# Weight preparation in 128-row chunks, half of it and the block-level work moved into the feed-forward loop

## The chip, the cores and the metric

The kernel runs on all 8 cores of one Trainium2 chip, each core on its own two sequences of a batch of 16. The metric is the device time of the slowest core in microseconds (us). No core talks to another.

## What is computed

One layer: attention by blocks plus a feed-forward part, both on the layer-normed input. Per sequence: 2048 tokens (2 to a core, so 4096 rows on it), 1024 channels, 16 heads of 64. Blocks are 32 tokens, so 64 x 64 block pairs for each head, of which about 1024 are computed exactly and the rest by block means ("low").

```python
xn = layernorm(x)
Q, K, V = (heads(xn @ W.T + b) for W, b in ...)        # Wq, Wk, Wv
Qh, Kh, Vh = block means of Q, K, V over 32 tokens
low  = Qh Kh^T * scale;  row_max = low.max(-1)
norm = low - row_max + band * 5000
thresh = value of the 1024th largest of norm           # per head and sequence
hi_mask = norm >= thresh
hi  : softmax parts over the selected block pairs, exact
low : exp(low - row_max - 10000 * hi_mask) * 32, with Vh
attn = (hi_out * hi_corr + low_out * low_corr) / (norms + 1e-6)

xr, xk = mu * xn + (1 - mu) * shift(xn)                # mu_r, mu_k
ffn = sigmoid(xr @ Wr.T) * (square(relu(xk @ Wk2.T)) @ Wv2.T)
out = x + attn + ffn
```

## The kernel before

The program is one list of instructions in order of emission. `emit` puts an instruction on an engine's queue; for every engine but TensorE (PE) it first adds a wait for that engine's own last instruction. So VectorE (DVE) and ScalarE (ACT) run without overlap of their own, and the DMAs of one queue (SyncE's, SP, or GpSimd's, POOL) go one at a time: each waits until the one before it has landed. `wait` adds a wait for another engine's count. `barrier` makes every engine wait for all.

The stages, in the order of the trace:

1. **Layer norm** (L215 to L270): 32 tiles of 128 rows, transposed by PE into xnT, which holds all 4096 tokens of the core with channels on partitions.
2. **Weight preparation** (L274 to L331). DVE sums xnT over blocks (L275, eight reductions; L279 scales them into xnh). Then for each of the six weights: one POOL load of the whole matrix into wbuf (L286, f32 in DRAM, bf16 in SBUF), 64 PE transposes in groups of eight into two PSUM tiles (L295), a DVE copy after each group (L301), eight SP stores of 256 KB to the scratch wT_sc (L308). For q, k and v the block means are projected with the transposed weight while it is in SBUF: per d eight matmuls (L316) and a bias by DVE (L324), one group at a time. The next load waits for the last store.
3. **Block-level attention** (L345 to L401). For each of 32 heads and sequences: two small matmuls and five DVE instructions (low scores, L351 to L368), then a transpose, a copy and a memset (vhp, L379 to L384). Then 64 POOL transfers of 8 KB lay norm_all out over 128 partitions (nb128, L390 and L393), for which DVE waits.
4. **FFN with bisection** (loop `for Q in range(8)`, L537). One Q is 512 tokens. It has three passes, r, k2 and v2, of eight slices d; a slice is eight matmuls of 512 columns (L516) with a 256 KB weight slice that SP loads into a ring fW (`load_wslice`, L509). `wload(i)` waits until the slice that last used the buffer is through PE. Before the r and k2 passes DVE computes the mix (`mu_mix`, 12 us), after them ACT (sigmoid) or DVE (relu) takes the results; after the k2 pass ACT squares (L588); after the v2 pass PE transposes and POOL stores the result to part_sc (L614 to L626), and a barrier ends the Q. The threshold is found by 58 iterations of a bisection (`emit_bisect_iter`, L404 to L434: twelve DVE instructions with one PE sum in the middle), four after each mix, until they are used up in Q = 7.
5. **Selection masks** (`emit_sel_all`), and then the **attention** itself (from L640), 3.6 ms of it.

The lines that order a pass:

```python
                    r.wait("tensor", "sSY", wst["ld"][gi])
                    if d == 0:
                        r.wait("tensor", "sDV", ndv_mixr)
                    r.wait("tensor", "sAC", cons[par])
                    npe_q = mm_quarter("r", fA, d, fW[gi % 4], par)
                    wst["mm"][gi] = npe_q
                    wload(gi + 4)
```

Of the kernel before, what the change touches and what calls it, by code (L numbers as in the profile page):

```python
# [10 lines left out]
BF = mybir.dt.bfloat16  # L11
AF = mybir.ActivationFunctionType
ALU = mybir.AluOpType
# [82 lines left out]
def build_program(debug=False, trunc=None):  # L96
# [36 lines left out]
    with stack:  # L133
# [72 lines left out]
        with contextlib.ExitStack() as st_p0:  # L206
# [75 lines left out]
            st_w = contextlib.ExitStack()  # L282
            wbuf = st_w.enter_context(nc.sbuf_tensor("wbuf", [128, 8 * C], BF))
            wTsb = st_w.enter_context(nc.sbuf_tensor("wTsb", [128, 8 * C], BF))
            for tag in ("q", "k", "v", "r", "k2", "v2"):
                nld = r.emit("gpsimd", lambda e, s=w_in[tag]: e.dma_start(  # L286
                    wbuf.rearrange("p (a c) -> p a c", a=8),
                    s.rearrange("(a p) c -> p a c", p=128)))
                r.wait("tensor", "sGP", nld)
                wcons = [0, 0]  # L290
                for dc in range(8):
                    wpt = pT2[dc % 2]
                    r.wait("tensor", "sDV", wcons[dc % 2])
                    for cc in range(8):
                        r.emit("tensor", lambda e, dc=dc, cc=cc, wpt=wpt: e.transpose(  # L295
                            wpt[:, cc * 128:(cc + 1) * 128],
                            wbuf[:, dc * C + cc * 128:dc * C + (cc + 1) * 128],
                            id_bf[:, :]))
                    npe_w = r.cnt["sPE"]
                    r.wait("vector", "sPE", npe_w)  # L300
                    wcons[dc % 2] = r.emit("vector", lambda e, dc=dc, wpt=wpt: e.tensor_copy(  # L301
                        wTsb.rearrange("p (cc d) -> p cc d", cc=8)[:, :, dc * 128:(dc + 1) * 128],
                        wpt.ap().rearrange("p (cc x) -> p cc x", cc=8)))
                r.wait("tensor", "sDV", r.cnt["sDV"])
                ndv_wT = r.cnt["sDV"]
                r.wait("sync", "sDV", ndv_wT)
                for d in range(8):
                    nst = r.emit("sync", lambda e, tag=tag, d=d: e.dma_start(  # L308
                        wT_sc[tag][d].rearrange("(cc p) j -> p cc j", p=128),
                        wTsb.rearrange("p (cc x) -> p cc x", cc=8)[:, :, d * 128:(d + 1) * 128]))  # L310
# [929 lines left out]
```

How the kernel before makes its waits and increments, by code:

```python
    def emit(self, eng, fn):  # L57
        sname = ESEM[eng]
        n = 16 if eng in ("sync", "gpsimd") else 1
        if eng != "tensor" and self.cnt[sname]:
            self.wait(eng, sname, self.cnt[sname])
        self.cnt[sname] += n
        h = self.sem[sname]
        self._push(eng, lambda e, fn=fn, h=h, n=n: fn(e).then_inc(h, n))
        return self.cnt[sname]
# [1 line left out]
    def wait(self, eng, sname, val):  # L67
        if not val:
            return
        h = self.sem[sname]
        self._push(eng, lambda e, h=h, v=val: e.wait_ge(h, v))
```

## Time and profile before

| | us |
|---|---|
| median of the runs shown (5599.2 and 5612.5) | 5605.8 |
| the profiled execution | 5611.8 |
| its span, slowest core | 5610.2 |
| spans of the eight cores | 5577.4 to 5610.2 |
| busy in that span: PE, DVE, ACT, POOL | 3104.9, 2488.8, 1712.3, 286.4 |
| DMA moved | 181.7 MB, mean 32 GB/s |

The profiled execution is one execution; its span goes from the first to the last instruction of the slowest core. Each core's mean granted TensorE clock was 0.755 to 0.763 of full speed. In the rows below PE is TensorE's matmuls, PEld its weight loads, SPq the issues of SyncE's DMA queue, L and a number a line of the kernel. A row that groups several instructions of a queue gives the time from the first to the last of them.

### The profile page before, as it was taken

Reading aid. Unit: us, or ns where it says so; the run is one execution under the profiler, and the core shown is the slowest. Engines: PE = TensorE matmul, PEld = TensorE weight load, DVE = VectorE, ACT = ScalarE, POOL = GpSimd, SP = SyncE. Lnnn points to the kernel's source line nnn. Section 1 sums busy time; section 2 is a strip of 40 time slices with the busy share of each in tenths; the row PEclk is TensorE's granted clock in tenths of the full one; section 3 lists DMA queues with packets and bytes.
Section 4 is the critical chain, followed back from the end, with each engine's and each line's share of the span. In section 5 each row is a group of like instructions: output and inputs, shape, how many; then the busy total and the mean of one; then the engine's idle time right before and its main releaser. Section 6 shows DMA issues by size and latency. Waiting matters only on the chain.

```text
span 5610.2 us, 57324 instructions; the slowest of 8 cores (5577.4 to 5610.2 us)
## 1 busy us (share of the span) xinstructions
PE 3104.9 (55%) x11513; PEld 1106.3 (20%) x11513; DVE 2488.8 (44%) x5263; ACT 1712.3 (31%) x2627; POOL 286.4 (5%) x301
## 2 busy tenths in 40 slices
PE   1121203333333426776777776776776776777776
PEld 0011101111111111222222222222222122222122
DVE  3431304444444323653653653652752752743643
ACT  2300000000000002453453454354354355355245
POOL 0000020000000000000000000000000000000000
PEclk9965556666666766887787787788788788688678
DMA  1244001111222211100100100110110110110110
GB/s 59 64 75 89 24 4 38 45 47 47 49 53 53 57 42 27 29 18 19 31 18 12 35 18 16 28 24 16 23 29 15 25 29 13 26 29 4 29 21 16
DMA packets 516779, 181.70 MB, mean 32 GB/s; under 512 B 494282, under 2 KB 495474, under 8 KB 516274
## 3 DMA queue, kind: packets, MB, share of 16 engines
q1 hardware_dynamic: 482386, 130.46, 10.2%
q0 software_dynamic: 34080, 47.56, 4.7%
q8 instruction: 135, 2.21, 0.2%
q14 instruction: 178, 1.46, 0.1%
HBM read 142.23 MB, written 39.34 MB: 32 GB/s over the span
## 4 chain that ended last, share of the span: by engine, by line
PE 36%; DVE 22%; DMA 15%; ACT 13%; issue 10%; DVEq 1%; ACTq 1%; POOL 0%; POOLq 0%; SPq 0%
PE pS L850 9%; DVE bm L776 8%; ACT aT L865 7%; PE pO L818 7%; PE pA L765 7%; PE pA L1011 4%; PE pA L516 3%; PE pA L1072 2%; ACT stage L946 2%; DMA nb<-norm_all 2%; DMA fW<-wT_v 2%; DVE fA L501 2%; DMA fW<-wT_k 1%; DVE bis_ge L409 1%; DVE bis_cnt L413 1%
## 5 line engine op out<-in xcount | busy, mean ns | idle before, releaser
L776 DVE TENSOR_REDUCE bm<-pA 128x16 f32<-128x512 f32 x1664 | 1151.2, 692 | 608.4 <-PE pA L765 474.2
L865 ACT ACTIVATE aT<-pS 128x1024 bf16<-128x1024 f32 x1024 | 1049.7, 1025 | 775.5 <-PE pS L850 734.7
L818 PE MATMUL pO<-aT,vtm 128*65 128x512 bf16 x2048 | 702.6, 429 | 309.4 <-ACT aT L865 308.7
L765 PE MATMUL pA<-ktp,qtp 64*128 64x512 bf16 x1664 | 685.1, 423 | 311.1 <-ACT aT L865 110.1
L850 PE MATMUL pS<-rhsc,lhsc 128*128 128x512 bf16 x2048 | 718.0, 440 | 0.0
L516 PE MATMUL pA<-fA,fW 128*128 128x512 bf16 x1536 | 392.8, 419 | 147.0 <-DVE bis_hi L434 45.5
L417 PE MATMUL pB<-bis_cnt,ones 128*128 128x32 f32 x116 | 35.2, 397 | 688.3 <-DVE bis_cnt L413 688.3
L818 PEld LDWEIGHTS pO<-aT,vtm 128*65 128x65 bf16 x2048 | 234.8, 122 | 648.2 <-issue 500.0
L776 DVE TENSOR_REDUCE bm<-pO 128x16 f32<-128x512 f32 x384 | 265.6, 692 | 212.0 <-PE pO L765 177.2
L765 PEld LDWEIGHTS pA<-ktp,qtp 64*128 64x128 bf16 x1664 | 152.1, 95 | 880.7 <-issue 876.8
L1072 PE MATMUL pA<-xnT,wsl_v 128*128 128x512 bf16 x512 | 160.6, 470 | 136.5 <-DMA out<-stage 131.0
L765 PE MATMUL pO<-ktp,qtp 64*128 64x512 bf16 x384 | 188.4, 519 | 84.5 <-DMA bx<-bsm_dram 59.9
L516 PEld LDWEIGHTS pA<-fA,fW 128*128 128x128 bf16 x1536 | 157.8, 106 | 376.6 <-issue 241.4
L850 PEld LDWEIGHTS pS<-rhsc,lhsc 128*128 128x128 bf16 x2048 | 160.5, 107 | 316.0 <-issue 279.5
L558 ACT ACTIVATE fR<-pA 128x512 bf16<-128x512 f32 x64 | 38.3, 598 | 588.0 <-PE pA L516 588.0
L558 ACT ACT_TABLE_LOAD x1 | 1.3, 1283 | 605.4 <-PE pA L516 605.4
L588 ACT ACTIVATE fA<-fB 128x512 bf16<-128x512 bf16 x64 | 40.4, 631 | 422.8 <-DVE fB L581 417.7
L417 PEld LDWEIGHTS pB<-bis_cnt,ones 128*128 128x128 f32 x116 | 29.1, 311 | 697.3 <-issue 697.3
L888 DVE TENSOR_TENSOR rdenw<-pS,eps_all 128x8 f32<-128x8 f32 x16 | 2.7, 167 | 366.4 <-PE pS L881 365.5
L1011 PE MATMUL pA<-xnT,wsl_q 128*128 128x512 bf16 x512 | 123.0, 386 | 67.2 <-DMA wsl_v<-wT_v 65.7
L946 ACT ACTIVATE stage<-pA,rdenw 128x64 f32<-128x64 f32 x384 | 121.5, 316 | 67.7 <-DVE rdenw L936 34.2
L785 DVE TENSOR_TENSOR bmm<-bm,bx 128x64 f32<-128x64 f32 x512 | 115.6, 226 | 54.2 <-DVE bm L776 1.4
(150 smaller groups left out, 2536.3 us busy)
## 6 DMA issues: line engine op xcount, KB each, us to landing
xtile<-x SPq DMA_DIRECT2D x64, 512.0 KB
fW<-wT_r SPq DMA_DIRECT2D x64, 256.0 KB
fW<-wT_k SPq DMA_DIRECT2D x64, 256.0 KB
fW<-wT_v SPq DMA_DIRECT2D x64, 256.0 KB
out<-stage SPq DMA_DIRECT2D x32, 512.0 KB
rhsc<-qtp POOLq DMA_DIRECT2D x32, 256.0 KB, 3.5
lhsc<-ktp POOLq DMA_DIRECT2D x32, 256.0 KB, 2.9
bx<-bsm_dram POOLq DMA_DIRECT2D x32, 256.0 KB, 7.8
```

The lines of the kernel that those rows point to most:

```text
L417: npe_c = r.emit("tensor", lambda e: e.matmul(pB1[:, :], ones128[:, :], bis_cnt[:, :], start=True, stop=True))
L501: e.scalar_tensor_tensor(d[:, c * QT:(c + 1) * QT], xnT[:, base:base + QT], mucol[m][:, c:c + 1], d[:, c * QT:(c + 1) * QT], ALU.mult, ALU ...
L516: e.matmul(pA[:, sl * 512:sl * 512 + QT], w[:, cc * 128:(cc + 1) * 128], rb[:, cc * QT:(cc + 1) * QT], start=(cc == 0), stop=(cc == 7)))
L765: e.matmul(pap, qtp[p0:p0 + 64, ts0 + t * 128:ts0 + (t + 1) * 128], ktp[p0:p0 + 64, ts0 + kq * 512:ts0 + (kq + 1) * 512], start=True, stop ...
L776: e.tensor_reduce(bmp[:, kq * 16:(kq + 1) * 16], pap.rearrange("p (k e) -> p k e", e=32), axis=AX.X, op=ALU.max))
L785: e.tensor_tensor(bmm[:, :], bmp[:, :], bx2[bpar][:, t * 64:(t + 1) * 64], ALU.add))
L818: e.matmul(pO[0:65, sl * 512:(sl + 1) * 512], vtm[:, (sq * 16 + k) * 130 + hip * 65: (sq * 16 + k) * 130 + hip * 65 + 65], aT[bpar][:, sl ...
L850: e.matmul(pS[bpar][:, sl * 512:(sl + 1) * 512], lhs2[par][:, k * 128:(k + 1) * 128], rhs2[par][:, qh * 1024 + sl * 512: qh * 1024 + (sl + ...
L865: e.activation(aT[bpar][:, :], pS[bpar][:, :], AF.Exp, scale=0.125))
L946: e.activation(stg[:, i * 64:(i + 1) * 64], pA[:, sl8 * 128:sl8 * 128 + 64], AF.Identity, scale=rdenw16[:, i:i + 1])))
L1011: e.matmul(pA[:, slot * 512:(slot + 1) * 512], wsl[tag][:, cc * 128:(cc + 1) * 128], xnT[:, cc * T + n * 512:cc * T + (n + 1) * 512], star ...
L1072: e.matmul(pA[:, slot * 512:(slot + 1) * 512], wsl["v"][:, cc * 128:(cc + 1) * 128], xnT[:, cc * T + n * 512: cc * T + (n + 1) * 512], sta ...
```

## The change

Three things are edited, all in stages 2 to 4.

- The whole-matrix buffers wbuf and wTsb give way to two chunk buffers wbuf2 and one wTsb2, each 128 x 1024. `wpd_load` loads 128 rows of a weight on POOL; `wpd_proc` transposes them, copies, stores the slice to wT_sc and, for q, k and v, projects the block means with it. Only r, k2 and v2 are now prepared ahead of the FFN, and the barrier behind the preparation is gone.
- q, k, v, the low blocks, the vhp blocks, nb128 and the bisection are put in a list of 24 sites, three in each Q: `do_site(Q * 3)` behind the r pass, `+ 1` behind the k2 pass, `+ 2` behind the v2 pass and its stores, ahead of the barrier. Sites 2 to 13 prepare two chunks each, 11 to 14 compute eight low blocks each, 15 all vhp blocks and nb128, 16 to 23 eight iterations of the bisection each (23: the last two).
- The ring fW has three buffers instead of four, and prefetches run three slices ahead.

```diff
+            def wpd_load(tag, d):
+                g = wp["g"]
+                wp["g"] = g + 1
+                r.wait("gpsimd", "sPE", wp["npe"].get(g - 2, 0))
+                wp["nld"][(tag, d)] = r.emit(
+                    "gpsimd", lambda e, tag=tag, d=d, g=g: e.dma_start(
+                        wbuf2[g % 2][:, :], w_in[tag][d * 128:(d + 1) * 128, :]))
...
+            def wpd_proc(tag, d):
+                nld, g = wp["nld"][(tag, d)]
                 r.wait("tensor", "sGP", nld)
...
+                r.wait("tensor", "sAC", r.cnt["sAC"])
                 r.wait("tensor", "sDV", r.cnt["sDV"])
+                wpt = pT2[g % 2]
...
+                npe_w = r.cnt["sPE"]
+                wp["npe"][g] = npe_w
+                r.wait("vector", "sPE", npe_w)
+                r.wait("vector", "sSY", wp["nst"])
+                nwc = r.emit("vector", lambda e, wpt=wpt: e.tensor_copy(
+                    wTsb2[:, :], wpt[:, :]))
+                r.wait("sync", "sDV", nwc)
+                wp["nst"] = r.emit("sync", lambda e, tag=tag, d=d: e.dma_start(
+                    wT_sc[tag][d].rearrange("(cc p) j -> p cc j", p=128),
+                    wTsb2.rearrange("p (cc x) -> p cc x", cc=8)))
                 if tag in ("q", "k", "v"):
...
+                r.wait("tensor", "sDV", r.cnt["sDV"])
+
+            for tag in ("r", "k2", "v2"):
+                wpd_load(tag, 0)
+                wpd_load(tag, 1)
+                for d in range(8):
+                    wpd_proc(tag, d)
+                    if d + 2 < 8:
+                        wpd_load(tag, d + 2)
...
             fW = [st_p0.enter_context(nc.sbuf_tensor(f"fW{j}", [128, 8 * 128], BF))
-                  for j in range(4)]
+                  for j in range(3)]
...
-                if i - 4 >= 0:
-                    r.wait("sync", "sPE", wst["mm"][i - 4])
+                if i - 3 >= 0:
+                    r.wait("sync", "sPE", wst["mm"][i - 3])
                 tag, d = wsched[i]
-                wst["ld"][i] = load_wslice(fW[i % 4], tag, d)
+                wst["ld"][i] = load_wslice(fW[i % 3], tag, d)
...
+            for j, tag in enumerate(("q", "k", "v")):
+                base = 2 + j * 4
+                for ch in range(4):
+                    for d2 in (0, 1):
+                        d = ch * 2 + d2
+                        addw(base + ch,
+                             lambda tag=tag, d=d: wpd_proc(tag, d))
+                        if d + 2 < 8:
+                            addw(base + ch,
+                                 lambda tag=tag, d=d: wpd_load(tag, d + 2))
+                nxt = {"q": "k", "k": "v", "v": None}[tag]
+                if nxt is not None:
+                    addw(base + 3, lambda nxt=nxt: wpd_load(nxt, 0))
+                    addw(base + 3, lambda nxt=nxt: wpd_load(nxt, 1))
+            for j, si in enumerate((11, 12, 13, 14)):
+                for bb in bh_list[j * 8:(j + 1) * 8]:
+                    addw(si, lambda bb=bb: emit_low_bh(*bb))
+            for bb in bh_list:
+                addw(15, lambda bb=bb: emit_vhp_bh(*bb))
+            addw(15, emit_nb128)
+            for si in range(16, 24):
+                for it in range((si - 16) * 8, (si - 16) * 8 + 8):
+                    if it < N_BISECT:
+                        addw(si, lambda it=it: emit_bisect_iter(it))
...
+            wpd_load("q", 0)
+            wpd_load("q", 1)
+            r.wait("vector", "sPE", r.cnt["sPE"])
             for Q in range(8):
                 t0 = Q * QT
                 mu_mix(fA, "r", t0)
                 ndv_mixr = r.cnt["sDV"]
-                for itq in range(4):
-                    it = Q * 8 + itq
-                    if it < N_BISECT:
-                        emit_bisect_iter(it)
...
-                    npe_q = mm_quarter("r", fA, d, fW[gi % 4], par)
+                    npe_q = mm_quarter("r", fA, d, fW[gi % 3], par)
                     wst["mm"][gi] = npe_q
-                    wload(gi + 4)
+                    wload(gi + 3)
...
+                do_site(Q * 3 + 0)
                 r.wait("vector", "sPE", r.cnt["sPE"])
                 mu_mix(fA, "k", t0)
```

`emit_low_bh`, `emit_vhp_bh` and `emit_nb128` hold the instructions of L345 to L401 as they were; the first two begin with PE waits for everything that ACT and DVE have been given so far.

## Rows read from the trace of the kernel before

**Rows 1.** The page: its span line, and the chain that ended last, by engine.

```profile
span 5610.2 us, 57324 instructions; the slowest of 8 cores (5577.4 to 5610.2 us)
...
PE 36%; DVE 22%; DMA 15%; ACT 13%; issue 10%; DVEq 1%; ACTq 1%; POOL 0%; POOLq 0%; SPq 0%
```

**Rows 2.** Windows by stage: stretch, then busy us per engine, clock, DMA share, GB/s.

```profile
284.70:594.10 309.40, 59.81 (x576) 47.96 (x576) 77.72 (x82) 0.00 (x0) 5.32 (x6) 0.62 0.44 82
594.10:845.40 251.30, 30.02 (x160) 19.89 (x160) 43.34 (x226) 0.00 (x0) 33.49 (x64) 0.50 0.03 7
845.40:2001.40 1156.00, 446.15 (x1908) 201.53 (x1908) 505.46 (x1142) 79.95 (x129) 15.73 (x29) 0.69 0.21 49
2001.40:5610.20 3608.80, 2535.86 (x8608) 811.49 (x8608) 1759.37 (x3484) 1547.92 (x2369) 231.03 (x197) 0.79 0.11 22
```

**Rows 3.** Timeline of w_k's preparation: start us, us, engine, line, instruction, [idle before].

```profile
370.53 1.01 PE L295 MATMUL pT<-id_bf,wbuf 128*128 128x128 bf16 x8 [28.33 <-DMA wbuf<-w_k]
...
378.60 19.58 SPq L308 DMA_DIRECT2D wT_k<-wTsb  x8
...
401.08 0.87 POOL L286 DMA_DIRECT2D wbuf<-w_v  x1 [47.73 <-DMA wT_k<-wTsb]
```

**Rows 4.** Timeline of TensorE and ScalarE in the first r and k2 passes.

```profile
884.26 14.61 PE L516 MATMUL pA<-fA,fW 128*128 128x512 bf16 x56 [3.17 <-DVE bis_hi L434]
...
956.33 1.89 PE L516 MATMUL pA<-fA,fW 128*128 128x512 bf16 x8 [1.22 <-DMA fW<-wT_k]
...
959.29 5.69 ACT L588 ACTIVATE fA<-fB 128x512 bf16<-128x512 bf16 x8 [57.02 <-DVE fB L581]
```

**Rows 5.** Timeline of SyncE's queue, same r pass: first and last of five issues.

```profile
887.97 0.36 SPq L509 DMA_DIRECT2D fW<-wT_r  x1
...
899.46 0.36 SPq L509 DMA_DIRECT2D fW<-wT_k  x1
```

**Rows 6.** Timeline at the borders: block means done, low blocks, vhp blocks, first mix.

```profile
321.02 0.69 DVE L279 TENSOR_SCALAR xnh<-sq_dump 128x1024 bf16<-128x1024 f32 x1
...
594.17 0.44 PE L351 MATMUL pA<-khT,qhT 64*64 64x64 f32 x2 [23.10 <-DMA wT_v<-wTsb]
...
673.73 0.28 PE L379 MATMUL pA<-id_f,vhT 64*64 64x64 f32 x1 [1.81 <-DVE rm_all L368]
...
845.45 0.06 DVE L487 MEMSET fA<- 128x1 bf16 x1 [138.73 <-DMA nb<-norm_all]
```

**Rows 7.** DMA issues: destination<-source, queue, count, KB each, us to landing.

```profile
wbuf<-w_k POOLq DMA_DIRECT2D x2, 2048.0 KB, 17.5
...
wbuf<-w_q POOLq DMA_DIRECT2D x1, 2048.0 KB, 17.4
...
nb<-norm_all POOLq DMA_DIRECT2D x64, 8.0 KB, 1.6
```

**Rows 8.** Timeline after the first v2 pass, and the landing of ptile's stores.

```profile
994.13 0.69 DVE L622 COPY ptileb<-pTb 128x1024 bf16<-128x1024 bf16 x1 [2.60 <-DMA part_sc<-ptileb]
...
1000.47 0.35 DVE L496 TENSOR_SCALAR fA<-xnT,mucol1m_r 128x512 bf16<-128x512 bf16 x1 [5.64 <-DMA part_sc<-ptileb]
...
DMA to landing us min/median/max: 2.3/2.5/4.2
```

**Rows 9.** Timeline of one group of head matmuls and its bias.

```profile
341.19 1.01 PE L316 MATMUL pA<-xnh,wTsb 128*128 128x128 bf16 x8 [0.68 <-DVE qhT L324]
342.38 0.35 DVE L324 TENSOR_SCALAR qhT<-pA,bcol_q 128x128 f32<-128x128 f32 x1 [1.33 <-PE pA L316]
```

**Rows 10.** Timeline: first instruction of two bisection iterations that follow each other.

```profile
870.77 0.19 DVE L405 TENSOR_TENSOR bis_mid<-bis_lo,bis_hi 128x32 f32<-128x32 f32 x1
...
877.21 0.19 DVE L405 TENSOR_TENSOR bis_mid<-bis_lo,bis_hi 128x32 f32<-128x32 f32 x1
```

**Rows 11.** Windows: the end of a k2 pass, and the head matmuls of w_k.

```profile
953.00:958.30 5.30, 3.77 (x16) 1.42 (x16) 1.08 (x2) 0.00 (x0) 0.00 (x0) 1.00 0.41 95
382.00:391.00 9.00, 5.35 (x43) 3.89 (x41) 1.85 (x6) 0.00 (x0) 0.00 (x0) 0.50 0.39 101
```

More of the change, by code:

```diff
@@ L280, in build_program @@
                 xnh[:, :], sq_dump[:, :], 1.0 / BLK, None, ALU.mult))
[L282 to L288, printed above, removed]
-                r.wait("tensor", "sGP", nld)
[L290 to L303, printed above, removed]
-                r.wait("tensor", "sDV", r.cnt["sDV"])
[L305 to L310, printed above, removed]
@@ new lines, in build_program @@
+            wbuf2 = [st_p0.enter_context(nc.sbuf_tensor(f"wbuf{j}", [128, C], BF))
+                     for j in range(2)]
+            wTsb2 = st_p0.enter_context(nc.sbuf_tensor("wTsb2", [128, C], BF))
+            wp = {"nld": {}, "npe": {}, "nst": 0, "wc": [0, 0], "g": 0}
+            def wpd_load(tag, d):
[5 more added lines that the diff above has]
+                        wbuf2[g % 2][:, :], w_in[tag][d * 128:(d + 1) * 128, :]))
+                wp["nld"][(tag, d)] = (wp["nld"][(tag, d)], g)
@@ L328, in build_program @@
-                r.wait("gpsimd", "sSY", nst)
-                r.wait("gpsimd", "sDV", r.cnt["sDV"])
-            r.barrier()
-            st_w.close()
+                    r.wait("tensor", "sDV", max(ndvh, nwc))
+                    for cc in range(8):
+                        r.emit("tensor", lambda e, cc=cc: e.matmul(
+                            pA[:, 0:128],
+                            wTsb2[:, cc * 128:(cc + 1) * 128],
+                            xnh[:, cc * 128:(cc + 1) * 128],
+                            start=(cc == 0), stop=(cc == 7)))
@@ new lines, in emit_nb128 @@
+            def emit_nb128():
+                ndv_n = r.cnt["sDV"]
+                r.wait("gpsimd", "sDV", ndv_n)
+                for b in range(NBH):
+                    r.emit("gpsimd", lambda e, b=b: e.dma_start(
+                        nb128[0:64, b * 32:(b + 1) * 32],
+                        norm_all[0:64, b * 64:b * 64 + 32]))
+                    r.emit("gpsimd", lambda e, b=b: e.dma_start(
+                        nb128[64:128, b * 32:(b + 1) * 32],
+                        norm_all[0:64, b * 64 + 32:b * 64 + 64]))
+                ngp_n = r.cnt["sGP"]
+                r.emit("vector", lambda e: e.memset(bis_lo[:, :], -100000.0))
+                r.emit("vector", lambda e: e.memset(bis_hi[:, :], 100000.0))
+                r.wait("vector", "sGP", ngp_n)
@@ L563, in build_program @@
                 ndv_mixk = r.cnt["sDV"]
-                for itq in range(4, 8):
-                    it = Q * 8 + itq
-                    if it < N_BISECT:
-                        emit_bisect_iter(it)
                 consd = [r.cnt["sDV"], r.cnt["sDV"]]
```

143 lines of the change are left out of this document (68 added, 75 removed).

## The prediction

> **What bounds the kernel now.** I read the spans and clocks of all cores first (5577 to 5610 us, one clock, so nothing is disturbed), then the busy times by stage, then the timeline of the first 2000 us, and the issues of SyncE's DMA queue last. The span is 5610.2 us, and no engine fills it: the chain that ended last is PE 36%, DVE 22%, DMA 15%, ACT 13% [rows 1]. By stage [rows 2]: from 284.7 to 594.1 the weights are prepared, to 845.4 stands the block-level attention, to 2001.4 the feed-forward part (FFN) with the bisection, and the last 3609 us are the attention, which the change does not touch. So at most about 1.7 ms is in play. Up to 2001 us this is a serial chain: every engine waits for its own last instruction, and at most steps for another engine. A piece of work that is moved costs as much in the new place, unless it finds there something to lie beside.
>
> The preparation is a case of waiting on transfers: of the 48.6 us from one load to the next (the idle 47.7 and the issue 0.9) some 18 are the load, 8 transposes and copies, 20 the eight stores [rows 3]. In the FFN, by contrast, a pass of 64 matmuls is already close to its weight loads. In the pass at 884.26 the first slice (8 matmuls) takes 3.7 us at half clock, and only then is its buffer free and the fifth slice's load issued; the following five issues (first and last shown) stand 2.87 us apart, in the next pass 3.0; the last slice starts after a DMA wait of 1.2 us [rows 4, 5]. With P = 2.95 us a load, the model 3.7 + 4 x 2.95 + 0.1 + 1.9 = 17.5 us gives the pass; 884.26 to 901.5 is 17.3, 940.4 to 958.2 is 17.8. All 24 passes end in this way.
>
> **The change, part by part.**
>
> (a) r, k2 and v2 are prepared by 128-row chunks. It still begins when DVE has the block means, at 321.7, and before the change the whole preparation ends at 594.2: 272.5 us [rows 6]. Afterwards 24 chunks run as a pipeline. Two limits: the store loop (one wTsb2: the copy, 0.7, waits for the previous store to land; 19.6 us for eight stores are 2.74 each [rows 3]) gives 3.6 us a chunk. The load loop (POOL, one at a time): the full load lands in 17.5 us and an 8 KB one in 1.6 [rows 7], so an eighth is 1.6 + 15.9/8 = 3.6, plus 0.5 issue, 4.15. POOL's stores beside other traffic took up to 4.2 us to landing where 2.5 is the median [rows 8]; the chunks run beside the stores, so up to 1.5 more. I take 4.5, between 3.6 and 5.65. 1.3 + 22 x 4.5 + 1.9 = 102 us, so the FFN begins at about 424. The term is -170 (-191 to -145).
>
> (b) q, k and v go to 12 sites in the FFN, two chunks each. One chunk on the chain: transposes 1.2 until the copy, copy 0.7, 0.25 to the head matmuls, 1.2 to the bias, 0.35, and 0.15 back: 3.8 us [rows 3, 9]. But the second copy waits for the first chunk's store, and this is queued on SyncE behind the last three weight prefetches. When a pass ends, the first of these has been in flight for 2 us; the store is issued at +6.9 and lands at +9.7; copy, matmuls and bias bring the site's end to +12.3. After the r pass DVE began the next mix at +0.2, so each of those four sites costs 12.1. After the k2 pass the squares began 1.1 us after its end [rows 4]; ACT now waits for the site: 11.3, four times. After the v2 pass PE's wait for DVE lets the site begin only after the last copy at 994.8; the prefetches are through by then, and the two chunks end at 1002.6 instead of the mix at 1000.5 [rows 8]. Behind them on POOL are the last store and two chunk loads of 4.15 each, for which the end-of-Q barrier waits: 1008.6, so 8.1, three times; at the fourth the low blocks cover the loads: 2.1. Sum: 48.4 + 45.2 + 24.3 + 2.1 = +120.
>
> (c) The 32 low blocks (2.49 us each, 594.17 to 673.73), the vhp blocks and the 64 nb128 transfers (138.7 us of DVE waiting [rows 6]) are moved, at nothing gained: PE waits for everything before them, and DVE stands before the k mix of Q = 5 just as it stood before Q = 0. What would cover nb128 is other DVE work, and there is none behind it in the queue. Only at the one v2 site that holds low blocks alone do they lie beside the last store, which took 5.6 us [rows 8]: -5. One second wait, for the last sigmoid: +1. Term -4.
>
> (d) The 58 iterations stay, 6.43 us each [rows 10]. They move from "behind the mix" to "behind the pass". After an r pass DVE's first four instructions (3.2 us) run during the pass (two sites); after a v2 pass 5.6 us of store lie under them (three sites); eight groups for fifteen save some hand-overs. -27.
>
> (e) The ring of fW goes from four buffers to three. By the model above slice 3 is now the first to wait for the end of slice 0: five loads instead of four stand between the first slice and the last. Each pass is P = 2.95 longer, and what follows each pass waits for its end: 24 x 2.95 = +71. Lower bound 0, if loads became quicker; upper in the rivals.
>
> The removed barrier is worth nothing. Sum: -170 + 120 - 4 - 27 + 71 = -10. Against the profiled execution's own time (5611.8 us, 1.6 us outside its span) that is 5602; it stood 6 us above the median of the runs shown, 5605.8, so I say 5596.
>
> The trace also bears on what a chunk load costs by rule: an 8 KB transfer on POOL took 1.6 us and the full load 17.5 [rows 7]. The Trainium skill, "DMA: Bandwidth & Descriptors" (Anatomy of one DMA), gives such a DMA about 2.0 us fixed and the bytes at 436 GB/s; for 512 KB that would be an estimated 3.2 us, the store loop would be the limit, and the sum -30 instead of -10. The full load by the same rule would be 11.6 us and took 17.5, so the rows decide.
>
> **Rivals.**
>
> *The clock falls in the thinned passes.* With three buffers PE works 1.75 us of each 2.95 us at the end of a pass, for four slices in a row instead of two. For: the head matmuls, 5.4 us busy in 9.0, ran at 0.50 of the clock throughout [rows 11]. Against: from 953.0 to 958.3, with two such gaps, it stayed at 1.00 [rows 11], and at the low clock a slice of 8 takes 3.41 us, which fills the interval, so it would rise again. If it falls once a pass: the last slice ends 1.9 later, 24 x 1.9 = +46, 5642. If from the fourth slice on all run at half clock, a pass takes 8 x 3.41 = 27.3 instead of 20.5: 24 x 6.8 = +163, 5759, slower by more than 2%. This is the case on the other side; it decides from +122, about 5 us a pass. The Trainium skill, "TensorE: Matmul & The Clock Gate" (HAM oscillation), describes just such a kernel, whose clock fell at every weight tile because PE waited for the next tile's transfer; the waits there were longer than the 1.2 us of these rows, and the trace does not agree so far.
>
> *The prefetch is not the limit.* If the loads ran closer together once there is one less in flight, (e) is worth 0: 5525. Against: they are already one at a time, each waiting for the one before. If besides the store of a site were not held up behind the prefetches (8 sites x 4.7 = 38), 5487, faster by over 2%.
>
> *The chunk loads are slow.* 6 us a load would put 33 us on the preparation and 3 x 3.7 on the barriers: 5640. Against: the two loads shown took 17.4 and 17.5, and the first of them (w_q) ran under DVE's block sums [rows 7]. The Trainium skill, "SBUF — State Buffer" (the "DVE blocks DMA" trap), says a DMA issued from GpSimd can be held up by some DVE instructions; no row here shows it.
>
> **How the numbers follow.** Forecast 0.60 (its own range 5565 to 5625: the bounds of (a)); clock once a pass 0.11; clock through the pass 0.06; ring free 0.08; ring and store free 0.08; slow chunk loads 0.07. A measurement of this kernel can tell about 2% (112 us) from no change. Faster by over 2%: 0.08. Slower: 0.06. Within: 0.86. The range leaves out the two outer cases: 5525 to 5650.
>
> **What would show it.** The timeline: the first r mix at 415 to 435, where it stood at 845.4. In each pass five prefetches about 2.95 apart before the last slice starts 18.6 us after the first; a pass takes 20.5. Granted clock 1.00 in the second half of passes. Weight sites of 12 us after r and k2 passes, with DVE's copy waiting for a wT store; at the end of Q 0 to 3 a barrier that waits for wbuf loads. DVE still idle 138.7 us for nb, now in Q = 5. The attention stage unchanged at 3609. I am wrong if passes stay at 17.6, if the clock is 0.5 late in passes, or if nb128 lies beside other work.

## The result, and the profile after

The changed kernel takes 5665.8 us (median; 5656.9 to 5670.2), the kernel before, run beside it, 5600.65. The ratio is 1.0112, 95% interval 1.0099 to 1.0124: slower by 1.1%. I had forecast a gain of 10 us (5596, range 5525 to 5650): the class "within 2%" holds, the sign and the range don't.

The profiled execution took 5657.2 us. First the page's span and chain, then the windows by stage (columns as in [rows 2]; the preparation, everything up to the masks, and the attention):

```profile
span 5655.6 us, 57782 instructions; the slowest of 8 cores (5626.3 to 5655.6 us)
...
PE 35%; DVE 22%; DMA 17%; ACT 14%; issue 11%; DVEq 1%; ACTq 1%; POOL 0%; SPq 0%; POOLq 0%
```

```profile
284.70:440.70 156.00, 24.27 (x192) 18.57 (x192) 52.14 (x33) 0.00 (x0) 13.77 (x26) 1.00 0.46 81
440.70:2080.80 1640.10, 528.15 (x2452) 248.44 (x2452) 575.38 (x1419) 79.76 (x129) 62.14 (x118) 0.66 0.19 44
2080.80:5655.60 3574.80, 2520.67 (x8608) 808.20 (x8608) 1757.84 (x3482) 1543.43 (x2369) 230.55 (x194) 0.79 0.11 22
```

The chain has more DMA than before (17% for 15%, [rows 1]) and less PE. All the difference is made by the moment at which DVE begins stage 5, "masks begin" from here on. Its row in the changed kernel's timeline:

```profile
2080.77 0.18 DVE L451 COPY thr<-bis_lo 128x32 f32<-128x32 f32 x1 [0.19 <-DVE bis_hi L446]
```

As the mean over the eight cores of each profile, masks begin at 2002.0 before and 2065.6 after: +64, as the times have it (+65). What is behind it lasts 3587 us before and 3576 after; over all the kernels below that figure lies between 3576 and 3593 in no order, so I take it for scatter. On core 5, which both profiles show, masks begin at 2011.9 and at 2080.8: +69, where my sum had -10. Its row in the kernel before:

```profile
2011.88 0.18 DVE L439 COPY thr<-bis_lo 128x32 f32<-128x32 f32 x1 [5.00 <-DMA part_sc<-ptileb]
```

[rows 2] puts the border at 2001.4, while the last copies and stores of the loop still run; the 3609 us that the prediction gives the attention hold 10.5 us of them. From masks to the end core 5 takes 3598 us before and 3575 after. Against the forecast 79 us have to be found, all of them in stages 2 to 4.

**The preparation** (answers to [rows 3, 6, 7]). Timeline of the changed kernel: start, us, engine, line, instruction, [idle before].

```profile
284.86 0.57 POOL L292 DMA_DIRECT2D wbuf<-w_r  x1 [282.61 <-DVE xnT L267]
289.56 0.54 POOL L292 DMA_DIRECT2D wbuf<-w_r  x1 [4.13 <-DMA wbuf<-w_r]
...
333.22 0.53 POOL L292 DMA_DIRECT2D wbuf<-w_r  x1 [4.62 <-DMA wbuf<-w_r]
333.75 0.69 DVE L311 COPY wTsb<-pT 128x1024 bf16<-128x1024 bf16 x1 [4.41 <-DMA wT_r<-wTsb]
...
440.72 0.06 DVE L499 MEMSET fA<- 128x1 bf16 x1
```

The first r mix is at 440.7, where I said 415 to 435. A chunk load alone leaves its queue idle for 4.13 us behind the issue (4.2 from the start of the issue to the landing), beside the stores for 4.6 to 4.8 (4.5 to 4.6 to the landing); that is a cycle of 5.1, not 4.5. DVE, too, waits 4.4 us for a store whose whole cycle was 2.7 when nothing ran beside it [rows 3]: the two loops slow each other and end up at the same pace.

**A pass** (answers to [rows 4, 5]). TensorE in the first k2 pass, then two windows of it, the pass at 485.86 and the tail of one at 1970 (columns as in [rows 2]):

```profile
485.86 9.45 PE L528 MATMUL pA<-fA,fW 128*128 128x512 bf16 x32 [12.46 <-DVE fA L513]
495.71 1.89 PE L528 MATMUL pA<-fA,fW 128*128 128x512 bf16 x8 [0.41 <-DMA fW<-wT_k]
498.73 1.89 PE L528 MATMUL pA<-fA,fW 128*128 128x512 bf16 x8 [1.12 <-DMA fW<-wT_k]
501.76 1.89 PE L528 MATMUL pA<-fA,fW 128*128 128x512 bf16 x8 [1.15 <-DMA fW<-wT_k]
504.88 1.89 PE L528 MATMUL pA<-fA,fW 128*128 128x512 bf16 x8 [1.23 <-DMA fW<-wT_k]
...
1975.25 3.36 PE L528 MATMUL pA<-fA,fW 128*128 128x512 bf16 x8 [2.43 <-DMA fW<-wT_k]
```

```profile
500.00:507.50 7.50, 4.39 (x19) 1.52 (x17) 1.94 (x3) 0.00 (x0) 0.00 (x0) 1.00 0.43 98
...
1975.25:1979.00 3.75, 3.36 (x8) 0.96 (x8) 0.21 (x1) 0.00 (x0) 0.00 (x0) 0.54 0.31 72
```

Four slices of this pass wait for their weights, spaced 3.0, and the clock stays at 1.00 (2.4 GHz) in these gaps: the tail of a pass is as drawn. The 24 passes last 508.6 us together, before 425.2: +83 where I had +71. Core 5 is the worst of the eight here; as the mean over the cores it is 500.7 for 425.0, +76. The slice at 1975.25 ran at a clock of 0.54 (the lower level), after a wait of 2.43 us, twice the usual. On this core one more late slice did, and one behind a wait as long did not:

```profile
1797.93 3.53 PE L528 MATMUL pA<-fA,fW 128*128 128x512 bf16 x8 [2.35 <-DMA fW<-wT_v]
...
1120.11 1.89 PE L528 MATMUL pA<-fA,fW 128*128 128x512 bf16 x8 [2.33 <-DMA fW<-wT_k]
```

**A weight site** (to be set against [rows 8, 9]). Between the r and the k2 pass of Q = 1; the pass ends at 590.87. The row with x3 holds the three prefetches.

```profile
588.81 9.63 SPq L521 DMA_DIRECT2D fW<-wT_k  x3
...
592.72 0.69 DVE L311 COPY wTsb<-pT 128x1024 bf16<-128x1024 bf16 x1 [22.72 <-PE pT L303]
593.08 0.53 POOL L292 DMA_DIRECT2D wbuf<-w_q  x1 [37.35 <-PE pT L303]
...
598.14 0.53 POOL L292 DMA_DIRECT2D wbuf<-w_q  x1 [4.53 <-DMA wbuf<-w_q]
602.98 3.90 SPq L314 DMA_DIRECT2D wT_q<-wTsb  x2
605.70 0.69 DVE L311 COPY wTsb<-pTb 128x1024 bf16<-128x1024 bf16 x1 [11.01 <-DMA wT_q<-wTsb]
```

The mechanism is the predicted one: DVE's second copy waits for the first chunk's store, and that stands behind three prefetches. But from the first prefetch (588.81) to the store (602.98) are 14.2 us, 4.7 each, where I had 2.95. The store is issued 12.1 after the pass, not 6.9. While a prefetch and a chunk load both move bytes, the DMA engines are nearly full. The DMA view from 593.2 to 598.1: 40 slices of 0.12 us, the busy share of the 16 engines in tenths (9 is 90% or more), and the share of GpSimd's queue over the whole window:

```profile
DMA  0000000026641034497897998999997899520000
...
q0 software_dynamic: 144, 0.26, 29.5%
```

**The moved block work** (answers to [rows 6]). A vhp block, and the first instruction of the k mix behind nb128:

```profile
1290.79 0.28 PE L389 MATMUL pA<-id_f,vhT 64*64 64x64 f32 x1 [0.94 <-DVE vhp_all L394]
...
1434.68 0.35 DVE L508 TENSOR_SCALAR fA<-xnT,mucol1m_k 128x512 bf16<-128x512 bf16 x1 [142.57 <-DMA nb<-norm_all]
```

DVE still stands idle for nb128, 142.6 us against 138.7, as said, in Q = 5. A vhp block takes 1.22 us instead of 1.01.

### The profile page after: what moved, and what is told of

Its sections match the earlier page's. It is cut to its first block, busy times and chain, and to the rows that moved or that the text cites. A ratio compares the mean times of both kernels' runs of the same rounds, so it can differ in the third digit from the quotient of the medians.

```text
span 5655.6 us, 57782 instructions; the slowest of 8 cores (5626.3 to 5655.6 us)
## 1 busy us (share of the span) xinstructions
PE 3106.1 (55%) x11513; PEld 1100.6 (19%) x11513; DVE 2488.9 (44%) x5263; ACT 1707.4 (30%) x2627; POOL 307.3 (5%) x343
## 4 chain that ended last, share of the span: by engine, by line
PE 35%; DVE 22%; DMA 17%; ACT 14%; issue 11%; DVEq 1%; ACTq 1%; POOL 0%; SPq 0%; POOLq 0%
PE pS L896 9%; DVE bm L822 8%; ACT aT L911 7%; PE pO L864 7%; PE pA L811 7%; PE pA L1057 4%; DMA fW<-wT_k 3%; DMA fW<-wT_v 3%; PE pA L1118 2%; ACT stage L992 2%; PE pA L528 2%; DMA fW<-wT_r 2%; DMA nb<-norm_all 2%; DVE fA L513 2%; DVE bis_ge L421 1%
## 5 line engine op out<-in xcount | busy, mean ns | idle before, releaser
L528 PE MATMUL pA<-fA,fW 128*128 128x512 bf16 x1536 | 405.1, 421 | 536.2 <-DVE fA L513 343.1
L1035 POOL TENSOR_TENSOR stage<-stage,xtile 128x1024 f32<-128x1024 f32 x32 | 74.9, 2340 | 1237.3 <-ACT stage L992 659.0
L836 DVE TENSOR_REDUCE mv_all<-bmm 128x1 f32<-128x64 f32 x512 | 112.7, 220 | 55.1 <-DVE bmm L831 3.0
```

Source lines behind the costliest of these rows:

```text
L528: e.matmul(pA[:, sl * 512:sl * 512 + QT], w[:, cc * 128:(cc + 1) * 128], rb[:, cc * QT:(cc + 1) * QT], start=(cc == 0), stop=(cc == 7)))
L836: e.tensor_reduce(mv_all[:, b * 16 + t:b * 16 + t + 1], bmm[:, :], axis=AX.X, op=ALU.max))
```

## The experiments

All compare with the kernel before run on the same chip. "Gap" is the time from the end of one pass to the start of the next. Passes and gaps are those of the core with the longest span in each profile; where the mean over the eight cores tells something else, it is given.

| | median us | ratio, 95% interval | masks begin, mean of cores | 24 passes, us |
|---|---|---|---|---|
| before | 5600.65 | 1 | 2002.0 | 425.2 |
| changed | 5665.8 | 1.0112 (1.0099 to 1.0124) | 2065.6 | 508.6 |
| e1 changed, ring of 4 | 5618.6 | 1.0006 (0.9981 to 1.0031) | 2019.0 | 428.7 |
| e2 before, ring of 3 | 5682.5 | 1.0125 (1.0089 to 1.016) | 2072.7 | 504.2 |
| e3 before, all six in chunks | 5586.7 | 0.9955 (0.9927 to 0.9984) | 1980.9 | 428.1 |
| e4 changed, stores first | 5645.1 | 1.0062 (1.0039 to 1.0085) | 2050.9 | 510.7 |
| e5 changed, ring of 4 and stores first | 5575.2 | 0.9928 (0.9893 to 0.9963) | 1965.7 | 451.6 |
| e6 before, nb128 by two DMAs | 5483.5 | 0.9783 (0.9749 to 0.9817) | 1874.0 | 435.1 |
| e7 as e3, 256 rows a load | 5585.8 | 0.9973 (0.9951 to 0.9995) | 1992.4 | 433.2 |
| e8 changed, fewer waits | 5655.7, one run | | 2056.0 | 509.4 |
| e9 before, with the gains of all | 5361.0 | 0.9543 (0.9456 to 0.963) | 1751.9 | 389.0 |
| e10 changed, with the same | 5391.6 | 0.9588 (0.9531 to 0.9645) | 1788.0 | 413.4 |
| e11 changed, chunk loads late | 5647.8 | 1.0084 (1.0058 to 1.011) | 2046.3 | 505.2 |
| e12 changed, q, k, v up front | 5625.7 | 1.0037 (1.0008 to 1.0067) | 2023.7 | 500.4 |

**e1 and e2: the ring alone.** xnrow2, idle in this stage, lends the changed kernel its fourth buffer; the kernel before gives one up.

```diff
-                    npe_q = mm_quarter("r", fA, d, fW[gi % 3], par)
+                    npe_q = mm_quarter("r", fA, d, fW[gi % 4], par)
                     wst["mm"][gi] = npe_q
-                    wload(gi + 3)
+                    wload(gi + 4)
```

> The changed kernel with four fW buffers again (the fourth is xnrow2, which is idle after the layer norm). Theory A (the shorter ring is the largest part of the loss: in the changed kernel 24 passes take 508.6 us against 425.2, one more transfer of about 3 us stands between the first and last slice of each): passes back to 17.6 us, the whole about 83 us shorter, 5580 to 5590, slightly faster than before. Rival B (the passes are longer because other transfers, chunk loads above all, now run beside the prefetches and slow each one): passes stay above 19.5, at most 20 us gained, 5645 or more.

> The kernel before with three fW buffers instead of four, nothing else. Theory A: each of 24 passes 3.0 to 3.4 us longer, 5672 to 5685. Rival B: with no chunk loads beside the passes they stay within 1 us of 17.7, at most 5625.

Measured: the ring is worth 70.7 us of masks in the kernel before (e2) and 46.6 in the changed one (e1). By the passes of the slowest cores it is 79 and 80, by their mean over the cores 74 and 71. e2's gaps are those of before within 2 us; e1's weight sites became longer: 29.0 to 31.5 us behind an r pass where the changed kernel has 28.0 to 28.8, and 24.4 to 25.3 behind a k2 pass where it has 21.4 to 22.1. Over the eight such sites that is 23 us as the mean over the cores, about what the masks of e1 (46.6) lack of its 71. A fourth prefetch stands ahead of the store. SyncE's queue in e1, whose pass ends at 578.54:

```profile
580.82 5.23 SPq L521 DMA_DIRECT2D fW<-wT_k  x2
588.66 0.36 SPq L521 DMA_DIRECT2D xnrow<-wT_k  x1
591.65 3.92 SPq L314 DMA_DIRECT2D wT_q<-wTsb  x2
```

The store leaves 13.1 after the pass, a further 1.0. So the ring's price is a buffer's worth of load per pass, and the queue order takes part of it back wherever something urgent stands behind the prefetches.

**e3 and e7: chunks without moving anything.** The kernel before, with all six weights through `wpd_load` and `wpd_proc` ahead of the FFN; e7 with 256 rows to a load.

```diff
-            for tag in ("q", "k", "v", "r", "k2", "v2"):
-                nld = r.emit("gpsimd", lambda e, s=w_in[tag]: e.dma_start(
-                    wbuf.rearrange("p (a c) -> p a c", a=8),
-                    s.rearrange("(a p) c -> p a c", p=128)))
...
+            order6 = [(tag, d) for tag in ("q", "k", "v", "r", "k2", "v2")
+                      for d in range(8)]
+            for i6, td in enumerate(order6):
+                wpd_proc(*td)
+                if i6 + 2 < len(order6):
+                    wpd_load(*order6[i6 + 2])
```

> The kernel before with all six weights prepared by 128-row chunks ahead of everything, as the changed kernel prepares three; ring of four, all else where it was. Theory A (a chunk costs one POOL load cycle of 5.15 us wherever it stands, and the move of q, k and v into the loop gained nothing, since a site of two chunks cost 15 to 18 us after r passes): 48 chunks in 250 us, the preparation ends near 570 where it ended at 594, about 5575. Rival C (the chunks of q, k and v are slower than 5.15 up front too, because the store, the head matmuls and the bias stand in line): 7 us for each of those 24, so it ends near 615, 5620.

> All six weights prepared up front in 128-row chunks, but loaded 256 rows at a time. Theory A (a load has a large fixed part: an eighth of a matrix took 4.1 us to land, the whole 17.5, so 2.2 fixed and 1.9 for each 128 rows): 6.0 us to landing, 6.6 a load or 3.3 for 128 rows, and the store loop and the head matmuls become the limit, 4.3 and 5 us a chunk; the low blocks begin 20 to 40 us sooner than with 128-row loads. Rival (time goes by rows and not by transfers): no difference, landing at 8.5 or more.

e3: masks 21 us earlier (the first pass 25 earlier as the mean over the cores, the passes together 7 longer). 48 chunks take 4.9 us each, where before the whole preparation was 5.7 us a chunk (272.5 / 48 [rows 6]); the loads land in 4.2 to 4.4. Its stores, by tile (ns shortest/median/longest, first and last start):

```profile
L315 SPq DMA_DIRECT2D wT_q<-wTsb x8: 359/359/387, 322.1 to 358.4; - x8
L315 SPq DMA_DIRECT2D wT_r<-wTsb x8: 359/360/360, 444.1 to 477.4; - x8
```

A chunk of w_q, with the projection of the block means, takes 5.2 us, one of w_r, without, 4.8: beside a load the projection costs 0.4.

e7's loads land in 5.8 to 6.0 us, 3.3 with the issue per 128 rows, and yet the preparation got no shorter: the first pass begins 11 us later than in e3 (mean over the cores), a chunk takes 5.2 us for 4.9. I had expected a gain of 20 to 40. The rows of e7 say why:

```profile
326.68 13.46 SPq L319 DMA_DIRECT2D wT_q<-wTsb  x3
...
334.71 0.69 DVE L316 COPY wTsb<-pT 128x1024 bf16<-128x1024 bf16 x1 [6.47 <-DMA wT_q<-wTsb]
```

The store issued at 326.68 holds up the copy until 334.71: 8.0 us for a store that alone takes 2.7. What the load loop gains, the store loop loses: the transfers of the two queues slow one another, and the pair keeps a pace near 5 us a chunk.

**e4 and e5: the prefetches behind the site's stores.**

```diff
+            def hold(d, i):
+                if d >= 8 - 3:
+                    held.append(i)
+                else:
+                    wload(i)
...
             def do_site(si):
                 for fn in site_work.get(si, ()):
                     fn()
+                for i in held:
+                    wload(i)
+                held.clear()
...
-                    wload(gi + 3)
+                    hold(d, gi + 3)
```

> The changed kernel, but the prefetches that a pass makes for the next one are put on SyncE's queue behind the site's stores, not ahead of them. Theory A (second chunk of a site waits for the first one's store, which is queued behind three prefetches): sites after r and k2 passes fall from 17.5 and 14.5 us to about 8.5 and 8.5, eight sites, 55 to 60 us in all if the later prefetches are still hidden, so 5605 to 5615. Rival D (the store itself is slow there because of the chunk loads beside it): at most 15 us gained, 5650.

> The changed kernel with four fW buffers, and with the prefetches behind the site's stores after r and k2 passes, not after v2 passes. Theory A (ring and queue order are independent: the ring gave 3.3 us a pass but made each site after r and k2 passes about 2 to 3 us longer, because one more prefetch stood before the store; with the order turned round the sites take 21 and 17 us from pass to pass): passes 17.9, 80 us, and eight sites 5 to 8 us each, about 50 us, so the masks begin at 1950 where they began at 2081, and the whole is 5535 to 5550. Rival E (the prefetches that are put back are then late for the next pass, and the passes grow by what the sites lost): masks at 2000, 5590.

e4's gaps fell to 21.0 to 21.5 behind r passes and 16.6 to 17.1 behind k2 passes, but rose from 36 to 42.5 behind v2 passes, where the barrier now waits for the prefetches too. Masks are only 15 us earlier: over the cores, 43 us are won at the r and k2 sites, 20 lost at the v2 sites and 8 in the passes. e5 leaves the v2 sites alone and adds the fourth buffer; its masks begin 100 us ahead of the changed kernel's, though its passes last longer than e1's (23 us on the slowest cores, 13 as the mean): the v2 passes of Q = 1 to 3, for which prefetches were held back at a short site, take 22 us. Even with the store first in the queue an r site costs 10.2 more than no site. The row in e4, whose first store was issued at 600.73:

```profile
600.73 6.38 SPq L314 DMA_DIRECT2D wT_q<-wTsb  x2
...
605.93 0.69 DVE L311 COPY wTsb<-pTb 128x1024 bf16<-128x1024 bf16 x1 [4.04 <-DMA wT_q<-wTsb]
```

5.2 us to the copy, with a chunk load issued at 600.27 beside it; in the changed kernel, whose second load (598.14, landing 4.5) was just through, it was 2.7 (602.98 to 605.70, above).

**e11: the chunk loads out of the way.** This tells two readings of the 4.7 us a prefetch apart: POOL's loads slow SyncE's queue, or the prefetches are slow by themselves. At the r and k2 sites both loads are emitted behind the two chunks, with this wait:

```diff
             def wpd_load(tag, d, late=False):
+                if late:
+                    r.wait("gpsimd", "sSY", wp["nst"])
```

> The changed kernel, but at the r and k2 sites the loads of the next two chunks wait until the site's second store has landed, so that nothing of GpSimd's queue moves while the prefetches and the site's first store are on SyncE's queue. Theory A (the sites cost more than predicted because the chunk loads and SyncE's transfers slow each other): the three prefetches behind a site stand about 3.0 apart instead of 4.7, the r sites' gap falls from 28.5 to about 23, the k2 sites' from 21.7 to about 18.5; in all about -35 us, of which the first prefetches of the next pass, now beside the loads, may give back 5 to 10: masks begin at 2031 to 2041 mean over the cores instead of 2066. Theory B (the prefetches behind a pass are slow by themselves): the gaps stay, masks begin at 2066.

SyncE's queue, then DVE, then GpSimd's queue in e11, whose pass ends at 589.36:

```profile
587.30 7.91 SPq L523 DMA_DIRECT2D fW<-wT_k  x3
597.87 3.91 SPq L316 DMA_DIRECT2D wT_q<-wTsb  x2
```

```profile
600.59 0.69 DVE L313 COPY wTsb<-pTb 128x1024 bf16<-128x1024 bf16 x1 [7.41 <-DMA wT_q<-wTsb]
```

```profile
604.62 0.53 POOL L294 DMA_DIRECT2D wbuf<-w_q  x1 [50.56 <-DVE fA L515]
609.01 0.53 POOL L294 DMA_DIRECT2D wbuf<-w_q  x1 [3.86 <-DMA wbuf<-w_q]
```

The prefetches stand 3.5 apart instead of 4.7, the r gaps fell from 28.5 to 24.4, the k2 gaps from 21.7 to 19.5, masks begin 19 us earlier. So the slowing is real and makes up most of the miss at these sites. Not all: 3.5 is not 2.95, and 24.4 is not 23. The rest sits in one place, which the single issues show. The second prefetch is issued at 593.21 in the changed kernel and at 591.87 in e11:

```profile
593.21 0.36 SPq L521 DMA_DIRECT2D fW<-wT_k  x1
...
591.87 0.36 SPq L523 DMA_DIRECT2D fW<-wT_k  x1
```

With the third (598.08 and 594.84) and the store, the intervals are 4.4, 4.9 and 4.9 in the changed kernel, 4.6, 3.0 and 3.0 in e11. Holding back the chunk loads gives the second and third prefetch their old 3.0 in full; the first is slow in both, and in both no chunk load has been issued when it starts (the changed kernel's comes at 593.08). What lies beside it is a transfer of 16 KB on a queue that the profile calls instruction. The DMA view from 588.81 to 593.21 in the changed kernel, then from 587.3 to 591.87 in e11:

```profile
q8 instruction: 1, 0.02, 2.2%
...
q8 instruction: 1, 0.02, 2.1%
```

At the r sites of Q = 1 to 3 this holds on all eight cores: first intervals of 3.9 to 5.1 us in the changed kernel and 4.0 to 5.0 in e11, with such a transfer in each; in e12 below the same prefetches have none beside them and take 2.8 to 3.1. The prefetches ahead of the waits of 2.33, 2.35 and 2.43 us above had one beside them too. No experiment moved this transfer, so its part is seen, not tested.

**e12: q, k and v back up front.** Part (b) undone alone.

```diff
-            for tag in ("r", "k2", "v2"):
+            for tag in ("q", "k", "v", "r", "k2", "v2"):
...
-                        addw(base + ch,
-                             lambda tag=tag, d=d: wpd_proc(tag, d))
```

> The changed kernel with q, k and v prepared by chunks ahead of the FFN together with r, k2 and v2, and nothing of them at the sites; ring of three, low blocks, nb128 and bisection as in the changed kernel. Theory A (a chunk in the loop costs 163/24 = 6.8 us as the gaps between the passes show, one up front 5.05 as in e3): 24 x 5.05 - 163 = -42, masks begin at about 2024 mean over the cores, time about 5624 us. Theory B (as I predicted: 120 us at the sites, against 24 x 4.5 = 108 up front): -12, masks at 2054, time 5654.

Masks at 2023.7, time 5625.7; theory A said 2024 and 5624. The first pass begins at 573.16 instead of 453.22, 5.0 us a chunk for 24 chunks. Moving the three weights into the loop costs 42 us more than it saves, two thirds of the whole slowdown. Without weights the gap behind a v2 pass is 25.4 to 26.4, with them 35.9 to 36.7.

**e6: nb128 by itself.** Two DMAs of 256 KB for the 64 of 8 KB.

```diff
-            for b in range(NBH):
...
+            for hf in range(2):
+                r.emit("gpsimd", lambda e, hf=hf: e.dma_start(
+                    nb128[hf * 64:(hf + 1) * 64, :].rearrange("p (b k) -> p b k", b=NBH),
+                    norm_all[0:64, :].rearrange("p (b k) -> p b k", b=NBH)
+                    [:, :, hf * 32:(hf + 1) * 32]))
```

> The kernel before with nb128 filled by two transfers in place of 64. Theory A (the 138.7 us are 64 times the fixed time of one transfer, 2.16 us, and the bytes are free): two transfers of 3 to 5 us, 130 us shorter, about 5485. Rival (small pieces are slow: 4096 pieces of 128 bytes take as long in two transfers as in 64): less than 60 us gained, 5555.

```profile
704.67 0.06 DVE L485 MEMSET fA<- 128x1 bf16 x1 [9.88 <-DMA nb<-norm_all]
```

```profile
nb<-norm_all POOLq DMA_DIRECT2D x2, 256.0 KB, 4.5
```

Idle 9.9 us instead of 138.7, masks 128 earlier, 2.2% faster. Moving this wait (the change) bought nothing; making it short is worth half of all that e9 below gains.

**e8: the waits in the blocks.** `emit_low_bh` and `emit_vhp_bh` give their two PE waits only in the first block of a site.

```diff
-                r.wait("tensor", "sAC", r.cnt["sAC"])
-                r.wait("tensor", "sDV", r.cnt["sDV"])
+                if (b % 8 if kind == "low" else b) == 0:
+                    r.wait("tensor", "sAC", r.cnt["sAC"])
+                    r.wait("tensor", "sDV", r.cnt["sDV"])
```

> The changed kernel without the two extra PE waits ahead of each low and vhp block, except at the first block of a site (the wait behind each block stays). Theory A (a wait costs PE time even when it is long fulfilled, some 0.1 us each): a vhp block takes 1.01 us again where it takes 1.22, a low block 2.47 instead of about 2.7, 13 us in all. Rival (the blocks are slower for another reason, the clock or the queue): no change.

```profile
1281.61 0.28 PE L391 MATMUL pA<-id_f,vhT 64*64 64x64 f32 x1 [0.73 <-DVE vhp_all L396]
```

A vhp block is back at 1.01 us, PE idle 0.73 for 0.94; masks 9.6 us earlier on the mean, in a single execution. The five gaps that hold blocks are 12 us shorter together (mean over the cores), which bears it out.

**e9 and e10: everything together, in place and moved.** e9 is the kernel before with chunks (e3), the two DMAs (e6), a ring of six, and four bisection iterations behind each r and each v2 pass. e10 is the changed kernel with e5, e6, e8 and a ring of five.

> The kernel before with four things put together: all six weights prepared by 128-row chunks up front (e3: 21 us earlier masks), nb128 by two DMAs (e6: 128 us earlier), a ring of six weight buffers (xnrow and xnrow2 lend their space; a pass had 5 loads at 2.95 between its first and last slice with three buffers and 4 with four, so two with six, and the pass is then bound by its matmuls: 3.7 + 7 x 1.9 = 17.0 instead of 17.6), and four bisection iterations behind the r pass and four behind the v2 pass in place of those behind each mix. Theory (each pass ends when its last load lands; a site costs what stands on the serial chain): masks begin at about 2002 - 21 - 128 - 24 x 0.6 to 24 x 2 - 27 = 1780 to 1812 mean over the cores, time 5365 to 5400 us. Rival (transfers share a limit, more prefetches in flight only slow the others, the chain is unchanged): the ring gives nothing, 1826, 5415.

> The changed kernel with its misses undone one by one: ring of five buffers, prefetches behind the sites' stores after r and k2 passes, nb128 by two DMAs, and the PE waits of low and vhp blocks given once a site instead of in each block. From e5 (masks begin 1966), nb128 -128, fewer waits -10, and one more buffer takes back part of the 23 us by which e5's passes were longer than e1's. Theory: masks begin at 1810 to 1828 mean over the cores, time 5415 to 5430 us, and so behind e9, because the q, k and v chunks in the loop cost 8 us or more each where up front they cost 5. Rival (moving work into the loop is as good as leaving it up front once prefetches are out of the way): the two kernels within 10 us of one another.

e9 is the best kernel of this study, 4.6% faster than before; its masks came 28 us earlier than the early end of what I expected. A pass now runs without a wait for weights (TensorE in e9, r pass at 700):

```profile
700.00 5.06 PE L527 MATMUL pA<-fA,fW 128*128 128x512 bf16 x16 [23.83 <-DVE bis_mid L416]
705.51 3.61 PE L527 MATMUL pA<-fA,fW 128*128 128x512 bf16 x16 [0.45 <-ACT fR L565]
708.96 3.62 PE L527 MATMUL pA<-fA,xnrow 128*128 128x512 bf16 x16
712.41 3.62 PE L527 MATMUL pA<-fA,fW 128*128 128x512 bf16 x16
```

I had 17.0 us for it; the mean is 16.2 (389.0 / 24), and this is 19 of the 28. e10, too, came earlier than I expected, by 22: its passes are 38 us shorter than e5's, where I had allowed 23. It stays 36 us of masks behind e9, every one of its cores (1780 to 1799) later than every one of e9's (1741 to 1774). Of the 36, 16 are longer passes (409 for 393 us as the mean over the cores; the v2 passes of Q = 1 to 3 take 22 again), 20 lie between the passes. So the moved kernel stays behind, but the two differ in the ring and in the places of the bisection as well, and no run tells what the moved weights alone cost here; that is told by e12.

## Why the prediction was wrong

The two largest terms, -170 and +120, and the ring's +71 nearly cancelled, so the sum of -10 was a small difference of large numbers, and four terms missed to the same side. On core 5, of 79 us:

| term | predicted | measured | miss |
|---|---|---|---|
| (a) first r mix | 424 | 440.7 | +17 |
| (b) r sites | 4 x 12.1 | 17.2, 18.0, 17.9, 17.5 | +22 |
| (b) k2 sites | 4 x 11.3 | 14.9, 14.2, 14.4, 13.2 | +11 |
| (b) v2 sites | 3 x 8.1 + 2.1 | about 38 in all | +11 |
| (c) vhp blocks and nb128 | 171.7 [rows 6] and 1 | 182.5 | +10 |
| (d) bisection | -27 | about -30 | -3 |
| (e) ring | +71 | +83 | +12 |

The misses add up to 80. The site costs are gaps of after less the same gap without weights (10.85 and 12.5 behind an r pass, 7.2 behind a k2 pass, 25.8 behind a v2 pass) and, in Q = 3 and 4, less 19.9 for eight low blocks; the v2 base is that of e12. With e12 as the base everywhere, eight low blocks cost 21.3 to 21.7 at the r and k2 sites, so 3 us of the r and k2 rows belong under (c), and the v2 row is 2 larger.

**The step that failed first** is in (b): "the store is issued at +6.9". It took the prefetch interval of a stretch in which nothing else moved [rows 5] and used it at a place where the change itself puts two chunk loads on the other queue. It was 12.1. e11 shows the cause: with those loads held back it is 8.5. Of the 5.2 us of miss, the two prefetches beside chunk loads make 3.8 (4.9 each for 3.0), and the first one, beside the instruction transfer, some 1.5. An estimate of what sharing alone must cost: between 593.2 and 598.1 the chunk load's packets take 29.5% of the 16 DMA engines' time, 1.4 us of all of them. I had allowed for stores making chunk loads slower (the 4.5 between 3.6 and 5.65), but not the reverse, and gave (b) no upper bound at all. Stores first in the queue (e4) recover 7 us at an r site and 5 at a k2 site from the other side. What is left of the miss after e11, 1.4 us at each r site, is that first prefetch; that the instruction transfer causes it is not shown. At the v2 sites I had the right wait, DVE's for the second wbuf load before the next mix, but at the first of them the two loads took 9.6 us for 8.3 and the last store 0.8 longer: 2 us for each of three sites. The rest of that row's miss is the site of Q = 3, not examined.

**(a)** came inside its bounds, at the upper half: the landing of an eighth, by the line through the 8 KB transfer and the full load, was to be 3.6 and is 4.2 alone. The small transfer was the wrong end of that line: it goes from SBUF to SBUF and needs no cast, and the slope between 128 rows (4.2 to 4.5) and 256 (5.8 to 6.0) gives an estimate of 2.5 to 3 us for the fixed part, not 1.6. The rule of the Trainium skill, "DMA: Bandwidth & Descriptors" (Anatomy of one DMA), from which I had estimated 3.2 us, agrees neither with this nor with the full load. Nor does the store loop keep its 3.6 us a chunk: beside chunk loads it takes 5.1 (a wait of 4.41 and the copy), and in e7 one store took 8.0 beside a large load.

**(e)** had the right model: five loads between the first slice and the last, four waits a pass, clock at 1.00. e2 gives 79, e1 80, where 24 x 2.95 is 71. As means over the cores, e2 gives 74, e1 71 and the change itself 76: the size was nearly right too, and 7 of the 12 us in the table are core 5. The interval is 3.0 in the pass shown, which makes 72; the rest is passes with some slower loads, such as the one at 1970 with its late slice at half clock. The sentence of (e) that each pass's price falls on everything behind it holds in e2 (masks +70.7), but not in e1, where a part came back at the sites.

**(c)** "at nothing gained" holds, and nb128 lies bare as forecast. That `emit_low_bh` and `emit_vhp_bh` begin with PE waits for work long done stood in the change's own text, and I priced it at nothing. By e8 it is 10 us over 64 blocks; 7 of them (32 x 0.21) are in this row, the rest in the low blocks under (b). The remaining 4 us are nb128's own 142.6 for 138.7, not examined.

**(d)** was right. (Two small slips change nothing: the bounds of (a) give 5575 to 5621, not 5565 to 5625, and a late slice keeps TensorE busy for 1.89 of 2.95 us, not 1.75.)

**The rivals.** The clock did not fall with the thinner passes: behind the second slice of a pass all but two slices of core 5 ran at full speed. Those two came after waits of 2.35 and 2.43 us, but one after 2.33 us kept its clock, so the length of the wait alone does not decide it. That the prefetch is not the limit is refuted by e1 and e2. "The chunk loads are slow" was half true, 5.1 a cycle between the 4.5 taken and the 6 of the rival, and a rival with both halves, loads slow and SyncE's queue slow beside them, would have been near: at 4.7 a prefetch instead of 2.95, eight sites cost 8 x 3 x 1.75 = 42 us more (measured 33, since the k2 sites' first prefetches were not slowed). The hold-up by DVE instructions that the Trainium skill names ("SBUF — State Buffer", the "DVE blocks DMA" trap) does not show in the two loads that ran beside DVE's work alone: the one at 284.86 ran under the block sums and landed in 4.2 us, e11's at 604.62 under the k mix and landed in 3.86, both sooner than the median of 4.5 beside stores. Two loads say nothing of other DVE instructions.

## What to carry to other kernels

Work moved into a loop to hide it must find idle transfers as well as idle engines: what runs on one DMA queue lengthens what runs on the other, however low the mean share of the DMA engines is, and an urgent store behind prefetches waits for all of them. When the terms of a sum are ten times the sum, each needs an upper and a lower bound with the change's own traffic in place, and errors of one cause (here: transfers side by side) add up. Before a long wait is moved, ask what it would take to make it short.

## What was new about the hardware

- A wait on PE that is already fulfilled is not free: two of them in each block cost 0.21 us (PE idle 0.94 for 0.73), 10 us over 64 blocks.
- Loads on POOL's queue and stores or loads on SyncE's slow each other although the mean share of the DMA engines is low (0.46 in the preparation): the mean counts the time in which a transfer moves nothing, and while both move the engines are 70% to over 90% busy (593.2 to 598.1). A store takes 2.7 us alone, 4.4 to 5.2 beside a 128-row load, up to 8.0 beside a 256-row load; a prefetch 2.95 alone, 4.9 beside a chunk load.
- A prefetch with one 16 KB transfer of an instruction queue beside it took 3.9 to 5.1 us at the r sites on all eight cores, 2.8 to 3.1 without; seen, not tested.
- 64 transfers of 8 KB took 138.7 us, two of 256 KB with the same bytes landed in 4.5 us each.
- Repeated waits of 1.0 to 1.2 us between slices left TensorE's clock at 1.00. After waits of 2.35 and 2.43 us the next slice ran at half speed, after one of 2.33 us at full speed.
